# Distance matmuls cut from 97 rows by 512 columns to four of 25 rows by 256 columns, x and y on row tiles of their own

## The chip, the cores and the metric

The kernel runs on one core of a Trainium2 chip. A core has TensorE (PE, with its weight loads shown apart as PEld), VectorE (DVE), ScalarE (ACT), GpSimd (POOL) and SyncE (SP, which here only issues DMAs). The metric is the device time of one execution in microseconds (us), as the median of several runs. The profile is one execution of its own, with its own time.

## The reference

The input is x of 4 images, 32x32 pixels, 128 channels. Three stages follow one another for every image, each added onto x:

```
x = x + conv(_gn(x))          # deformable convolution, 8 groups, 9 points, 32 channels per group
t = t + attn(_ln_t(t))        # slice attention over the 1024 tokens, 8 heads
t = t + ffn(_ln_t(t))         # top-2 of 8 experts, 128 -> 512 -> 128, gelu

# in conv, for each pixel, group g and point k:
px, py = ww + deform[..., 0], hh + deform[..., 1]
samp = gather(y0, x0) * wy0 * wx0 + gather(y0, x0 + 1) * wy0 * wx1 + ...   # 4 corners
out  = einsum('bhwgkc,bhwgk->bhwgc', samp, weights) @ out_w + out_b
```

## The kernel before, in words

The gather is done without addresses. For one set (a position in the token order together with a group) and a sampled point, the weight of grid column q is relu(1 - |px - q|), and the same for rows with py. So the kernel needs for every point its distance to each of the 32 grid lines, in x and in y. The step `distances(k)` makes these distances on PE: the positions, split into three bf16 parts whose sum is the f32 value, are the stationary operand (`lp`, 97 rows: 3 parts times 32 sets, and a row of ones), and a constant 0/1 matrix (`spread_b`, with minus the grid number in its last row, as 1 - q) is the moving operand. One matmul gives 16 sets times 32 grid lines for 128 points: one bank of PSUM (512 f32 columns). There is one for x (bank 4) and one for y (bank 5).

The work is a loop over 4 images x 8 groups x 4 batches x 2 halves, so k runs from 0 to 255. For each k:

- PE: `distances(k + 3)` (line 731), then side work, then `products(n, pair)` of k (line 743, 32 f32 matmuls of 36 rows x 64 columns, which the profile counts as 64), and after every eighth k `contract` (line 758, 128 f32 matmuls on 32x32 tiles, counted as 256); one k later `project` (line 766) of the group before.
- ACT: `take_x` (line 1031, reads bank 4), side work, two `x_ramps` (line 1041), which `products` waits for.
- DVE: `take_y` (line 1331, reads bank 5), side work, `take` (line 1339, copies the products out).
- POOL: two `ysb` products (line 655) from what `take_y` wrote.
- SP: `load_group` brings the next group's positions (line 452), weights (459) and values (466) from DRAM, where `store_parts` (439) put the positions of a whole image.

The side work is written out by hand by slot numbers (`PREP_SLOTS`, `ATTENTION_SLOTS`, `TILE_SLOT` and so on): under image 0's groups runs the preparation of images 1 to 3, under those of image 1 to 3 the attention and the experts of the image before. On PE it stands between `distances(k + 3)` and `products` of k, and nearly all of it is matmuls with 128 rows and 128 columns of weights. The last image's attention and experts follow the loop. Every engine runs its queue in order; semaphores tie them. Ahead of the loop stands a prologue in which POOL makes the constants (line 593 is the 0/1 pattern of `spread_b`) and DVE finishes them (1186, 1190); ACT starts only after them.

A "height" below is the tile height with which a matmul sets up the 128x128 array: with up to 32 rows, up to 64, or all 128.

Of the kernel before, what the change touches and what calls it, by code (L numbers as in the profile page):

```python
# [30 lines left out]
ALU = mybir.AluOpType  # L31
# [18 lines left out]
LROWS = PARTS * SETS + 1  # L50
# [90 lines left out]
def conv_attn_moe(nc, t_in, out):  # L141
# [3 lines left out]
    with ExitStack() as ctx:  # L145
        def sb(name, shape, dt=F32):
            return ctx.enter_context(nc.sbuf_tensor(name, shape, dt))
# [9 lines left out]
        parts_dram = nc.dram_tensor("position_parts", [B, PARTS, P, G * 2 * P], BF16, kind="Internal").ap()  # L157
# [47 lines left out]
        spread_b = sb("spread_b", [P, SETS, GRID], BF16)  # L205
# [50 lines left out]
        spread_f = early[:, N:2 * N].rearrange("p (s q) -> p s q", s=SETS)  # L256
# [123 lines left out]
        def _(sp):  # L380
# [56 lines left out]
            def store_parts(b):  # L437
                sp.wait_ge(s.parts_ready, b + 1)
                sp.dma_start(parts_dram[b].rearrange("r p n -> p r n"), parts).then_inc(s.parts_stored, 16)
# [5 lines left out]
            def load_group(ig):  # L445
# [5 lines left out]
                for r in range(PARTS):  # L451
                    sp.dma_start(lp[r * SETS:(r + 1) * SETS, ig % 2, :, :, :].rearrange("p b d n -> p b (d n)"),
                                 parts_dram[b][r].rearrange("(b p) (g n) -> g p b n", b=BATCHES, g=G)[g])\
                      .then_inc(parts_loaded[ig % 2], 16)
# [105 lines left out]
        def _(pl):  # L560
# [29 lines left out]
            for r in range(PARTS):  # L590
                if r:
                    pl.wait_ge(s.constants_made, 15 + r)
                pl.affine_select(out=spread_f, in_=spread_f, compare_op=ALU.not_equal, fill=1.0, base=-SETS * r,
                                 pattern=[[-1, SETS], [0, GRID]], channel_multiplier=1).then_inc(s.constants_made, 1)
            block_diagonal(head_mask, DH, 18)
            for q in range(4):
                if q:
                    pl.wait_ge(s.constants_made, 20 + q)
                v = head_pick[:, :].rearrange("p (j g) -> p j g", g=S)
                pl.affine_select(out=v, in_=v, compare_op=ALU.not_equal, fill=1.0, base=-32 * q,  # L600
                                 pattern=[[-S // HG, HG], [0, S]], channel_multiplier=1).then_inc(s.constants_made, 1)
# [67 lines left out]
        def _(pe):  # L669
# [52 lines left out]
            def distances(k):  # L722

                n, half = k // 2, k % 2
                ig, beta = n // BATCHES, n % BATCHES
                if beta == 0 and half == 0:
                    pe.wait_ge(parts_loaded[ig % 2], 16 * PARTS * (ig // 2 + 1))
                for d, bank, taken, done in ((0, X_BANK, s.x_taken, s.dx_summed), (1, Y_BANK, s.y_taken, s.dy_summed)):
                    if k:
                        pe.wait_ge(taken, k)  # L730
                    pe.matmul(ps[:, bank, :], lp[0:LROWS, ig % 2, beta, d, :],  # L731
                              spread_b[0:LROWS, half * CHUNK:(half + 1) * CHUNK, :].rearrange("p s q -> p (s q)"),
                              start=True, stop=True).then_inc(done, 1)
# [224 lines left out]
            pe.wait_ge(s.constants_made, 24)  # L958
# [197 lines left out]
        def _(dve):  # L1156
# [10 lines left out]
            def small_constants():  # L1167
                dve.memset(eps_col[:, :], EPS).then_inc(s.small_constants, 1)
                dve.wait_ge(s.constants_made, 18)
# [15 lines left out]
                last = PARTS * SETS  # L1185
                chain(s.small_constants, dve.tensor_scalar(
                    spread_f[last:last + 1, :, :],
                    grid_i[last:last + 1, :].rearrange("p (o q) -> p o q", o=1).broadcast_to([1, SETS, GRID]),
                    -1.0, 1.0, ALU.mult, ALU.add), 9)
# [448 lines left out]
```

## Time and profile before

| | |
|---|---|
| median of 3 runs | 1552.92 us (1536.53 to 1554.06) |
| profiled execution: its time, its span | 1547.26 us, 1544.8 us |
| PE busy, and mean granted clock | 1215.9 us (79%), 0.796 of 2.4 GHz |
| DVE, ACT, POOL busy | 904.8, 733.5, 693.5 us |
| chain that ended last | PE 61%, DVE 21%, issue 8%, POOL 5% |

The chain is the one to read for what a change is worth: it leads back from the last instruction, at each step to what released it. A busy share is only how much an engine had to do. The granted clock is 1.2 or 2.4 GHz at any moment, so the same instructions stand in the trace with two lengths.

### The profile page before, as it was taken

How to read it: one execution, taken by the hardware profiler on the slowest of the kernel's cores; microseconds unless marked ns; L12 is line 12 of the kernel's file. 1: busy time of each engine (PE TensorE's matmuls, PEld its weight loads, DVE VectorE, ACT ScalarE, POOL GpSimd, SP SyncE). 2: the span in 40 equal slices, each digit the busy share in tenths (PEclk: the TensorE clock that was granted, in tenths of full speed). 3: DMA queues.
4: the chain of work that ended last, by engine and by line, in shares of the span. 5: the costliest groups of instructions: out<-in, count | busy, mean ns of one | idle time of the engine just before them, and what ended most of it. 6: DMA issues, size and time to landing. Idle time of an engine off the chain costs nothing.

```text
span 1544.8 us, 63235 instructions
## 1 busy us (share of the span) xinstructions
PE 1215.9 (79%) x28236; PEld 943.8 (61%) x28236; DVE 904.8 (59%) x1619; ACT 733.5 (47%) x1403; POOL 693.5 (45%) x674
## 2 busy tenths in 40 slices
PE   3297785987898789998977889998877899865391
PEld 2165564665556568886565668875565688735291
DVE  4468578686768556446767454457785644464311
ACT  1255363553565256665553347665543566422060
POOL 4155455454443564347533744466335644420303
PEclk9568695795897668997996569997977899986596
DMA  5502213122000321552111224621103235200761
GB/s 137 136 25 52 79 40 78 60 58 79 25 27 22 88 83 58 149 146 68 30 35 44 68 69 124 182 86 42 38 11 98 73 108 163 83 18 0 243 178 53
DMA packets 166288, 121.96 MB, mean 79 GB/s; under 512 B 45641, under 2 KB 146050, under 8 KB 165506
## 3 DMA queue, kind: packets, MB, share of 16 engines
q1 hardware_dynamic: 161922, 109.53, 25.3%
q0 software_dynamic: 4096, 8.40, 1.8%
q8 instruction: 222, 3.64, 1.0%
q14 instruction: 48, 0.39, 0.1%
HBM read 89.38 MB, written 28.51 MB: 76 GB/s over the span
## 4 chain that ended last, share of the span: by engine, by line
PE 61%; DVE 21%; issue 8%; POOL 5%; ACT 2%; DMA 1%; SPq 0%; DVEq 0%; POOLq 0%; ACTq 0%
PE ps L743 15%; PE ps L758 14%; PE ps L731 7%; PE ps L918 5%; PE ps L931 5%; DVE asb L1339 4%; PE ps L766 3%; DVE yr L1331 2%; POOL ysb L655 1%; DVE x_tok L1348 1%; POOL picked L633 1%; DVE region L1297 1%; PE ps L787 1%; PE ps L841 1%; PE ps L696 1%
## 5 line engine op out<-in xcount | busy, mean ns | idle before, releaser
L655 POOL TENSOR_TENSOR ysb<-yr,rw 128x512 f32<-128x512 f32 x512 | 552.5, 1102 | 629.7 <-DVE yr L1331 549.9
L743 PEld LDWEIGHTS ps<-xsb,ysb 36*64 36x64 f32 x16384 | 324.6, 160 | 148.0 <-issue 120.5
L743 PE MATMUL ps<-xsb,ysb 36*64 36x64 f32 x16384 | 363.7, 249 | 58.0 <-DVE x_tok L1348 34.2
L1339 DVE COPY asb<-ps 128x1024 f32<-128x1024 f32 x256 | 312.3, 1220 | 163.3 <-PE ps L743 161.6
L1041 ACT ACTIVATE xsb<-xr,pick 128x512 f32<-128x512 f32 x512 | 361.7, 764 | 4.4
L1331 DVE TENSOR_SCALAR yr<-ps 128x512 f32<-128x512 f32 x256 | 174.3, 681 | 223.0 <-PE ps L731 217.6
L758 PE MATMUL ps<-asb,vd 32*32 32x256 f32 x8192 | 212.2, 465 | 63.4 <-DVE asb L1339 50.7
L731 PE MATMUL ps<-spread_b,lp 97*128 97x512 bf16 x512 | 190.4, 452 | 57.4 <-DVE yr L1331 28.6
L1031 ACT ACTIVATE xr<-ps 128x512 f32<-128x512 f32 x256 | 152.0, 594 | 172.5 <-PE ps L731 172.0
L758 PEld LDWEIGHTS ps<-asb,vd 32*32 32x32 f32 x8192 | 153.5, 114 | 116.1 <-issue 88.0
L1048 ACT ACTIVATE osp<-ps 128x256 f32<-128x256 f32 x128 | 39.6, 402 | 274.8 <-PE ps L758 274.8
L1116 ACT ACTIVATE region<-ps,b_col 128x128 f32<-128x128 f32 x368 | 105.4, 370 | 89.2 <-PE ps L918 89.2
L623 POOL DMA_INDIRECT sorted_rows<-region,row_no x64 | 62.9, 983 | 119.1 <-DVE row_no L1519 103.4
L633 POOL DMA_INDIRECT picked<-expert_rows,row_no x64 | 61.5, 960 | 91.3 <-DMA expert_rows<-region 74.5
L731 PEld LDWEIGHTS ps<-spread_b,lp 97*128 97x128 bf16 x512 | 32.7, 100 | 102.0 <-DVE yr L1331 38.2
L918 PEld LDWEIGHTS ps<-region,ring 128*128 128x128 f32 x616 | 81.3, 196 | 9.8 <-issue 1.6
L918 PE MATMUL ps<-region,ring 128*128 128x128 f32 x616 | 84.4, 281 | 1.5 <-issue 1.5
L931 PE MATMUL ps<-ring,region 128*128 128x128 f32 x616 | 82.5, 277 | 0.0
L931 PEld LDWEIGHTS ps<-ring,region 128*128 128x128 f32 x616 | 76.2, 194 | 0.4
L1557 DVE COPY region<-ps 128x128 f32<-128x128 f32 x92 | 26.8, 291 | 76.3 <-PE ps L931 76.3
L766 PEld LDWEIGHTS ps<-outw,osp 128*128 128x128 f32 x512 | 65.1, 200 | 6.5 <-ACT osp L1048 1.8
L766 PE MATMUL ps<-outw,osp 128*128 128x128 f32 x512 | 65.3, 283 | 1.3 <-ACT osp L1048 1.3
(232 smaller groups left out, 1097.4 us busy)
## 6 DMA issues: line engine op xcount, KB each, us to landing
ring<-in_L_ffn_W SPq DMA_DIRECT2D x154, 256.0 KB, 3.3
vd<-group_values SPq DMA_DIRECT2D x128, 128.0 KB, 2.7
asb<-in_L_ffn_W SPq DMA_DIRECT2D x30, 256.0 KB, 4.5
position_parts<-region SPq DMA_DIRECT2D x4, 1536.0 KB, 5.8
lp<-position_parts SPq DMA_DIRECT2D x96, 64.0 KB, 2.6
group_values<-region SPq DMA_DIRECT2D x32, 128.0 KB, 3.4
weight_rows<-region SPq DMA_DIRECT2D x4, 1024.0 KB, 4.3
rw<-weight_rows SPq DMA_DIRECT2D x32, 128.0 KB
```

What stands on the lines that cost most here:

```text
L655: pl.tensor_tensor(ysb[:, n % 2, pair * CHUNK:(pair + 1) * CHUNK, u, :], yr[:, k % 3, :, :], rw[:, ig % 2, u, first:first + CHUNK].rearran ...
L731: pe.matmul(ps[:, bank, :], lp[0:LROWS, ig % 2, beta, d, :], spread_b[0:LROWS, half * CHUNK:(half + 1) * CHUNK, :].rearrange("p s q -> p ( ...
L743: last = pe.matmul(o[:, :, NV * q:NV * q + NV], ysb[rows, n % 2, col, :, :].rearrange("p u y -> p (u y)"), xsb[rows, n % 2, col, :, :], st ...
L758: last = pe.matmul(ps[32 * jc:32 * jc + 32, j, 0:256], vd[rows, ig % 2, x, :], asb[rows, x, :, :, :].rearrange("p i n m -> p (i n m)"), st ...
L766: last = pe.matmul(pcol(2, t), osp[:, t, :], outw[:, ig % G, :], start=True, stop=True)
L918: last = pe.matmul(ps[:, hidden_bank(b, i), j * P:(j + 1) * P], ring_part(r, 0)[:, j * P:(j + 1) * P], xsT[:, i, :], start=True, stop=True)
L931: last = pe.matmul(ps[:, expert_bank(b, i), 0:C], hT[:, i % 2, j, :], ring_part(r, 1)[:, j * P:(j + 1) * P], start=(j == 0), stop=(j == HJ ...
L1031: act.activation(xr[:, half * CHUNK:(half + 1) * CHUNK, :].rearrange("p s q -> p (s q)"), ps[:, X_BANK, :], ACT.Relu, bias=1.0, scale=-1.0 ...
L1041: act.activation(xsb[:, n % 2, sets, :, v], xr[:, sets, :], ACT.Relu, bias=pick[:, v:v + 1], scale=-1.0).then_inc(s.x_ready, 1)
L1116: last = act.activation(hT[:, i % 2, j, :], ps[:, hidden_bank(b, i), j * P:(j + 1) * P], ACT.Gelu, bias=b1_col[:, i, j:j + 1])
L1331: dve.tensor_scalar(yr[:, k % 3, :, :].rearrange("p s q -> p (s q)"), ps[:, Y_BANK, :], 0.0, 1.0, ALU.max, ALU.min).then_inc(s.y_taken, 1)
L1339: dve.tensor_copy(asb[:, :, :, 2 * beta + pair, :].rearrange("p x i m -> p i x m"), ps[:, 2 * pair:2 * pair + 2, :].rearrange("p i (x m) - ...
```

## The change

Each pair of distance matmuls becomes four. x and y of a half of 16 sets no longer hold all 97 rows; each has a strip of 25 rows (8 sets x 3 parts and the row of ones) which starts at partition 0, 32, 64 or 96, and is multiplied by a 25-row constant into 256 columns. x and y of the same 8 sets stand in neighbouring strips, one behind the other in the queue, and write different banks. The positions lie in DRAM so that the three parts of a set are neighbours, and a group is loaded with eight DMAs of 24 partitions in place of three of 32. The constant is made for four strips (twelve selects of 256 columns in place of three of 1024).

```diff
-LROWS = PARTS * SETS + 1
+OCT = 8
+LROWS = 1 + PARTS * OCT
-        parts_dram = nc.dram_tensor("position_parts", [B, PARTS, P, G * 2 * P], BF16, kind="Internal").ap()
+        parts_dram = nc.dram_tensor("position_parts", [B, P, PARTS, G * 2 * P], BF16, kind="Internal").ap()
-        spread_b = sb("spread_b", [P, SETS, GRID], BF16)
+        spread_b = sb("spread_b", [P, OCT, GRID], BF16)
-                sp.dma_start(parts_dram[b].rearrange("r p n -> p r n"), parts).then_inc(s.parts_stored, 16)
+                sp.dma_start(parts_dram[b], parts).then_inc(s.parts_stored, 16)
-                for r in range(PARTS):
-                    sp.dma_start(lp[r * SETS:(r + 1) * SETS, ig % 2, :, :, :].rearrange("p b d n -> p b (d n)"),
-                                 parts_dram[b][r].rearrange("(b p) (g n) -> g p b n", b=BATCHES, g=G)[g])\
-                      .then_inc(parts_loaded[ig % 2], 16)
+                for half in range(2):
+                    for d in range(2):
+                        first = 32 * (2 * half + d) + 1
+                        for o in range(2):
+                            sp.dma_start(lp[first:first + PARTS * OCT, ig % 2, :, o, :],
+                                         parts_dram[b].rearrange("(b h o m) r x -> (b h o m r) x", h=2, o=2, m=OCT)
+                                         .rearrange("(b h o z) (g d n) -> h g d o z b n", h=2, o=2, z=PARTS * OCT, g=G,
+                                                    d=2)[half, g, d, o]).then_inc(parts_loaded[ig % 2], 16)
...
-            for r in range(PARTS):
-                if r:
-                    pl.wait_ge(s.constants_made, 15 + r)
-                pl.affine_select(out=spread_f, in_=spread_f, compare_op=ALU.not_equal, fill=1.0, base=-SETS * r,
-                                 pattern=[[-1, SETS], [0, GRID]], channel_multiplier=1).then_inc(s.constants_made, 1)
+            for i in range(4 * PARTS):
+                pl.wait_ge(s.constants_made, 15 + i)
+                pl.affine_select(out=spread_f, in_=spread_f, compare_op=ALU.not_equal, fill=1.0,
+                                 base=-(32 * (i // PARTS) + 1 + i % PARTS), pattern=[[-PARTS, OCT], [0, GRID]],
+                                 channel_multiplier=1).then_inc(s.constants_made, 1)
...
-                    pe.wait_ge(parts_loaded[ig % 2], 16 * PARTS * (ig // 2 + 1))
-                for d, bank, taken, done in ((0, X_BANK, s.x_taken, s.dx_summed), (1, Y_BANK, s.y_taken, s.dy_summed)):
-                    if k:
-                        pe.wait_ge(taken, k)
-                    pe.matmul(ps[:, bank, :], lp[0:LROWS, ig % 2, beta, d, :],
-                              spread_b[0:LROWS, half * CHUNK:(half + 1) * CHUNK, :].rearrange("p s q -> p (s q)"),
-                              start=True, stop=True).then_inc(done, 1)
+                    pe.wait_ge(parts_loaded[ig % 2], 16 * 8 * (ig // 2 + 1))
+                if k:
+                    pe.wait_ge(s.x_taken, k)
+                    pe.wait_ge(s.y_taken, k)
+                for o in range(2):
+                    for d, bank, done in ((0, X_BANK, s.dx_summed), (1, Y_BANK, s.dy_summed)):
+                        rows = slice(32 * (2 * half + d), 32 * (2 * half + d) + LROWS)
+                        last = pe.matmul(ps[:, bank, o * OCT * GRID:(o + 1) * OCT * GRID], lp[rows, ig % 2, beta, o, :],
+                                         spread_b[rows, :, :].rearrange("p s q -> p (s q)"), start=True, stop=True)
+                        if o:
+                            last.then_inc(done, 1)
...
-                last = PARTS * SETS
-                chain(s.small_constants, dve.tensor_scalar(
-                    spread_f[last:last + 1, :, :],
-                    grid_i[last:last + 1, :].rearrange("p (o q) -> p o q", o=1).broadcast_to([1, SETS, GRID]),
-                    -1.0, 1.0, ALU.mult, ALU.add), 9)
+                for row in range(0, P, 32):
+                    last = dve.tensor_scalar(spread_f[row:row + 1, :, :], across(grid_i, OCT)[row:row + 1, :, :],
+                                             -1.0, 1.0, ALU.mult, ALU.add)
+                chain(s.small_constants, last, 9)
```

The order of PE's queue where attention stands under image 1's groups. Before (L731 distances, L743 products, L766 the projection, L806 attention's projection, L823 and L824 its logits):

```order
L731 MATMUL ps<-spread_b,lp 128x512 [waits x_taken]
L731 MATMUL ps<-spread_b,lp 128x512 [waits y_taken]
L766 MATMUL ps<-outw,osp 128x128 [waits out_copied]
L766 MATMUL ps<-outw,osp 128x128 x7
L806 MATMUL ps<-wxT,region 128x256 [waits rtemp_ready]
L806 MATMUL ps<-wxT,region 128x256 x3
L743 MATMUL ps<-xsb,ysb 64x32x2 [waits conv_added,y_ready,x_ready]
L743 MATMUL ps<-xsb,ysb 64x32x2 x31
```

The same place now (L739 distances, L752 products, L775 projection, L815 attention's):

```order
L739 MATMUL ps<-spread_b,lp 128x256 [waits y_taken,x_taken]
L739 MATMUL ps<-spread_b,lp 128x256 x3
L775 MATMUL ps<-outw,osp 128x128 [waits out_copied]
L775 MATMUL ps<-outw,osp 128x128 x7
L815 MATMUL ps<-wxT,region 128x256 [waits rtemp_ready]
L815 MATMUL ps<-wxT,region 128x256 x3
L752 MATMUL ps<-xsb,ysb 64x32x2 [waits conv_added,y_ready,x_ready]
L752 MATMUL ps<-xsb,ysb 64x32x2 x31
```

Nothing has changed its place; two distance matmuls are four of half the columns, and the first of them carries both waits.

SP's queue at the first group, before:

```order
L439 DMA position_parts<-region 128x3x2048 [waits parts_ready]
L443 DMA weight_rows<-region 128x2048 [waits rows_copied]
L452 DMA lp<-position_parts 32x4x256 [waits parts_stored]
L452 DMA lp<-position_parts 32x4x256 x2
L459 DMA rw<-weight_rows 128x256 [waits rows_stored]
```

and now:

```order
L440 DMA position_parts<-region 128x6144 [waits parts_ready]
L444 DMA weight_rows<-region 128x2048 [waits rows_copied]
L456 DMA lp<-position_parts 24x4x128 [waits parts_stored]
L456 DMA lp<-position_parts 24x4x128 x7
L464 DMA rw<-weight_rows 128x256 [waits rows_stored]
```

Eight loads of positions stand ahead of the load of the weights, with 256 bytes in a row in place of 512.

## Rows read from the trace of the kernel before

**Rows 1.** The page: span, and busy time of each engine (share, instructions)

```profile
span 1544.8 us, 63235 instructions
PE 1215.9 (79%) x28236; PEld 943.8 (61%) x28236; DVE 904.8 (59%) x1619; ACT 733.5 (47%) x1403; POOL 693.5 (45%) x674
```

**Rows 2.** The page: the chain that ended last, by engine and line

```profile
PE 61%; DVE 21%; issue 8%; POOL 5%; ACT 2%; DMA 1%; SPq 0%; DVEq 0%; POOLq 0%; ACTq 0%
PE ps L743 15%; PE ps L758 14%; PE ps L731 7%; PE ps L918 5%; PE ps L931 5%; DVE asb L1339 4%; PE ps L766 3%; DVE yr L1331 2%; POOL ysb L655 1%; DVE x_tok L1348 1%; POOL picked L633 1%; DVE region L1297 1%; PE ps L787 1%; PE ps L841 1%; PE ps L696 1%
```

**Rows 3.** Chain in order of time (start us, us, what), 539 to 543 us

```profile
539.59 0.97 PE ps L731 x2
540.55 1.92 PE ps L743 x64
```

**Rows 4.** The same, 644 to 650 us

```profile
645.10 0.54 PE ps L731 x2
645.64 0.89 PE ps L918 x8
646.53 0.89 PE ps L931 x8
647.43 1.09 PE ps L743 x64
```

**Rows 5.** Chain, first and last pairs of the three commonest kinds, with what follows

```profile
112.15 0.54 PE ps L731 x2
112.69 0.49 PE ps L696 x2
...
1331.84 0.54 PE ps L731 x2
1332.38 0.89 PE ps L918 x8
...
1181.29 0.97 PE ps L731 x2
1182.25 0.85 PE ps L886 x4
...
79.07 0.97 PE ps L731 x2
80.04 1.92 PE ps L743 x64
...
1198.30 0.97 PE ps L731 x2
1199.27 0.74 PE ps L743 x19
```

**Rows 6.** Chain, one contraction

```profile
552.57 7.21 PE ps L758 x236
```

**Rows 7.** PE, 763 to 767 us (start, us, engine, line, operation, out<-in, shape, count)

```profile
763.91 1.13 PE L823 MATMUL ps<-region,ws_bd 128*128 128x512 f32 x2
764.96 1.12 PE L824 MATMUL ps<-region,head_pick 32*128 32x512 f32 x2
766.01 1.16 PE L743 MATMUL ps<-xsb,ysb 36*64 36x64 f32 x64
```

**Rows 8.** Chain, 411 us: four f32 matmuls of 512 columns at one height

```profile
411.08 1.72 PE ps L787 x4
```

**Rows 9.** PE, 860 to 862 us: a matmul of 8 rows behind the distances

```profile
860.09 1.04 PE L731 MATMUL ps<-spread_b,lp 97*128 97x512 bf16 x2
861.05 0.79 PE L892 MATMUL ps<-b,region 8*128 8x128 f32 x2
```

**Rows 10.** PE, 805 to 807 us: products behind the distances

```profile
805.90 0.60 PE L731 MATMUL ps<-spread_b,lp 97*128 97x512 bf16 x2
806.43 0.75 PE L743 MATMUL ps<-xsb,ysb 36*64 36x64 f32 x36
```

**Rows 11.** Line 731: idle time of PE and PEld ahead of it (us, times)

```profile
  DVE yr L1331: 66.8, 38
  ACT xr L1031: 35.4, 25
```

**Rows 12.** Who waited for whom (us, times, longest): products on ACT

```profile
PEld ps L743 <- ACT xsb L1041: 18.3, 20, 1.6
```

**Rows 13.** Timeline of the prologue, POOL and DVE, then ACT

```profile
1.39 0.30 POOL L565 MEMSET vbias<- 128x256 f32 x1
1.64 0.94 POOL L566 MEMSET asb<- 128x1024 f32 x1
9.92 4.09 POOL L593 TENSOR_SCALAR_AFFINE_SELECT asb<-asb 128x1024 f32<-128x1024 f32 x3
14.04 0.28 DVE L1170 CAST count<-asb 128x32 f32<-128x32 int32 x1 [13.09 <-POOL asb L593]
14.70 1.98 POOL L600 TENSOR_SCALAR_AFFINE_SELECT head_pick<-head_pick 128x128 f32<-128x128 f32 x4
15.75 0.77 DVE L1186 TENSOR_SCALAR asb<-asb 1x1024 f32<-1x1024 int32 x1
16.55 1.02 ACT L1000 ACTIVATE region<-ps 128x1024 f32<-128x1024 f32 x1 [6.69 <-DVE asb L1186]
```

**Rows 14.** Timeline, first two loads of positions and the first distances

```profile
64.45 2.48 SPq L452 DMA_DIRECT2D lp<-position_parts  x3
69.36 1.01 PE L731 MATMUL ps<-spread_b,lp 97*128 97x512 bf16 x2 [6.38 <-DMA lp<-position_parts]
70.65 1.37 SPq L452 DMA_DIRECT2D lp<-position_parts  x3
```

**Rows 15.** Line 452: who waited for it, and time to landing

```profile
  PE ps L731: 6.4, 1
DMA to landing us min/median/max: 1.9/2.6/5.8
```

**Rows 16.** Windows: length, busy us of PE, PEld, DVE, ACT, POOL, then PEclk, DMA share, GB/s

```profile
76.00:92.00 16.00, 16.00 (x344) 11.81 (x343) 10.75 (x16) 12.05 (x19) 11.88 (x12) 0.50 0.06 15
196.00:216.00 20.00, 17.23 (x489) 12.33 (x488) 19.35 (x30) 15.19 (x23) 13.88 (x14) 1.00 0.07 21
644.60:651.40 6.80, 6.80 (x176) 6.13 (x170) 4.22 (x6) 5.79 (x15) 2.97 (x3) 1.00 0.54 158
```

More of the change, by code:

```diff
@@ L255, in conv_attn_moe @@
         grid_i = early[:, 6 * G * K:6 * G * K + GRID].bitcast(I32)
-        spread_f = early[:, N:2 * N].rearrange("p (s q) -> p s q", s=SETS)
+        spread_f = early[:, N:N + OCT * GRID].rearrange("p (s q) -> p s q", s=OCT)
         at[0] = 0
@@ L588, in _ @@
             pl.memset(turn_flat, 0.0).then_inc(s.constants_made, 1)
-            for r in range(PARTS):
-                if r:
-                    pl.wait_ge(s.constants_made, 15 + r)
-                pl.affine_select(out=spread_f, in_=spread_f, compare_op=ALU.not_equal, fill=1.0, base=-SETS * r,
-                                 pattern=[[-1, SETS], [0, GRID]], channel_multiplier=1).then_inc(s.constants_made, 1)
-            block_diagonal(head_mask, DH, 18)
+            for i in range(4 * PARTS):
[3 more added lines that the diff above has]
+                                 channel_multiplier=1).then_inc(s.constants_made, 1)
+            block_diagonal(head_mask, DH, 27)
             for q in range(4):
                 if q:
-                    pl.wait_ge(s.constants_made, 20 + q)
+                    pl.wait_ge(s.constants_made, 29 + q)
                 v = head_pick[:, :].rearrange("p (j g) -> p j g", g=S)
@@ L957, in _ @@
                 prepare(0, step)
-            pe.wait_ge(s.constants_made, 24)
+            pe.wait_ge(s.constants_made, 33)
             pe.wait_ge(s.grid_chain, 2)
@@ L1168, in small_constants @@
                 dve.memset(eps_col[:, :], EPS).then_inc(s.small_constants, 1)
-                dve.wait_ge(s.constants_made, 18)
+                dve.wait_ge(s.constants_made, 27)
                 dve.tensor_copy(count[:, :], grid_i).then_inc(s.small_constants, 1)
```

## The prediction

> **What bounds the kernel now.** The busy shares come first [rows 1]: PE is busy 79% of the span and no other engine over 59%, so nothing but PE can be near its limit, yet a share says nothing of order. The chain of waits does [rows 2]: 61% of it is work of PE and 21% of DVE; the distance matmuls (L731) hold 7%, about 110 us. Read in order of time, the chain shows two speeds of the same step. At 538 us, where PE does only distances and products, a pair of distances takes 0.97 us and the products 1.92 [rows 3]; at 645 us, with the experts between, the pair takes 0.54 and the products 1.09 [rows 4]. The windows say why: the granted clock is 0.50 of full speed in the one kind of stretch and 1.00 in the other [rows 16].
>
> Followed piece by piece, the chain goes through 173 of the 256 pairs, and they differ by speed and by what stands behind them (the first and the last of each kind stand in [rows 5]): 120 pairs of 0.54 us ahead of a 128-row matmul, 26 of 0.97 ahead of such a one, 17 of 0.97 ahead of products. The other ten are 3 of 0.54 ahead of products, 1 of 0.54 and 2 of 0.97 ahead of the 8-row matmul L892, and 3 and 1 (by speed) where the chain leaves PE. What the change is worth depends on this list.
>
> **The columns.** A pair streams 1024 columns. At half the clock they take twice as long, so 0.97 - 0.54 = 0.43 us is their time at 2.4 GHz, and 0.11 is left, which the clock hardly moves [rows 3, 4]. The change streams as many columns, but x and y may run side by side: 512 column steps, if they do. That they do is likely. The 64 products, with halves of rows and of columns as tiles, take 1.09 us; eight 128-column f32 matmuls take 0.89, so 64 of 64 columns would take 3.6 one by one [rows 4]: more than three run at once. In a contraction 256 matmuls of 256 columns take some 7.3 us (236 recorded in 7.21), where one by one they would need 256 x 0.22 = 56 [rows 6]: over seven at once, and one strip of 32 rows has only four tiles of 32 columns, so strips overlap too. So a pair gets shorter by 0.21 us at 2.4 GHz and 0.43 at 1.2; its ends are 0 (one after the other) and these.
>
> **The change of height.** Against this stands something that the diff does not show. Before, the distances have 97 rows and the array is set up for 128, as for nearly all the side work behind them; the side work's first weights are loaded under the distances. Now the distances are set up for 32 rows, and the array is set up anew before the side work. The trace has this step in attention: L824 has 32 rows and stands behind L823 with 128. From L823 to L824 it is 1.05 us, from L824 to the products again 1.05 [rows 7]. Each is two passes of 512 columns, and four such passes at one height take 1.72 [rows 8], two 0.86: each of the two changes of height costs 0.19 us, weights not loaded ahead among it. At 1.2 GHz I take 0.30, between 0.19 and twice that; the 8-row matmul there starts 0.96 us after the distances, 0.10 over the two passes' 0.86, and its own weights then take time too [rows 9]. Ahead of products nothing is added: from distances to products the height changes today as well (0.53 us at 2.4 GHz, 0.10 over the columns) [rows 10]. Nor from products to distances.
>
> Sum over the chain: 120 x (0.21 - 0.19) = 2.4; 26 x (0.43 - 0.30) = 3.4; 20 slow pairs without a new change (17, 2, 1) x 0.43 = 8.6; 7 fast ones x 0.21 = 1.5. Together **16 us gained**. The ends: with no charge for the height 127 x 0.21 + 46 x 0.43 = 46 gained; without overlap 120 x 0.19 + 26 x 0.30 = 31 lost. Off the chain the shorter pairs are worth nothing.
>
> **The waits.** The x matmul now waits for `take_y` as well. y held up the queue before, so PE stands as long as ever (66.8 us for DVE ahead of line 731) [rows 11]; but ACT gets x later in these cases, and with it `take_x`, its side work and the ramps, which are needed three steps on. Products waited 18.3 us for ACT in all [rows 12]. I take 2 us lost, ends 0 and 10. y is there 0.2 us sooner after the pair starts, which helps DVE where it waits; that is in the shortened pairs already.
>
> **Prologue.** POOL made three selects of 1024 columns in 4.09 us (1.36 each) and four of 128 in 1.98 (0.50 each) [rows 13]: 0.97 ns per column and 0.37 fixed, so twelve of 256 take 12 x 0.62 = 7.4, 3.3 more. The memset of the same tile falls from 0.94 to about 0.30, as for another tile of 256 columns. DVE's row of ones becomes four short instructions (0.77 us together, perhaps 1.0). ACT's first copy waits for all this, and the preparation for ACT: **2.8 us later** (0 to 4). Then the first distances wait for the positions. Five more issues at 1.37 / 3 = 0.46 us [rows 14] are 2.3 us; the first three took 0.83 each, which is the upper end, 4.1; if the last lands no sooner, all of it counts. I take **2.3**. Later groups load about a group ahead, and PE waited for this load once only, at the start [rows 15], so SP's five further issues in each of 31 groups are hidden by it; if a load were late, each group would pay some 2 us.
>
> The positions now move in rows of 256 bytes in place of 512. The Trainium skill ("DMA: Bandwidth & Descriptors", Specifications) states that below 512 bytes a DMA engine reads, modifies and writes. By that the first landing of 2.6 us would be longer, perhaps doubled by an estimate from the row, and the sum 2.6 us more; no row here shows such a load of positions, and I leave it out.
>
> **The clock.** From 76 to 92 us PE never pauses, with products, distances and little else, and is granted 0.50; from 644 to 651 it never pauses either, with the experts' 128-row matmuls in it, and is granted 1.00; from 196 to 216, with the preparation woven in, it is granted 1.00 at 17.2 busy of 20 [rows 16]. So the low clock goes with narrow work, not with pauses alone, and the change makes the distances narrow: 25 rows in place of 97. Stretches that hold 2.4 GHz today with preparation or attention may lose it. If the one from 196 to 216 did, its 17.2 busy us would be 34.4 in place of 20: 14 us. I take one such, **14 us lost**, with 0 and three (43) as ends.
>
> **The sum.** 1547.3 (the profiled execution's own time, span 1544.8) - 16 + 2 + 5 + 14 = 1552.3. That execution lies 5.7 below the median of the three runs; their spread of 17.5 us is wider than this, and I make no correction. **Forecast 1552 us: no change.** A change of 2% (31 us) is about what a measurement of this kernel can tell.
>
> **Rivals.**
>
> 1. The change of height costs nothing here, and the clock holds. For it: between distances and products a change of height costs only 0.10 us [rows 10], so side work might pay as little or less. Against it: L824 pays it twice in [rows 7]. Then 1547 - 46 + 2 + 5 = 1508, faster by 2.6 to 2.9%. Chance 0.13. The Trainium skill ("TensorE: Matmul & The Clock Gate", Measured speedup vs the span model) gives 3.07 times for four 32-row tiles side by side and no charge for what stands between; by it alone this rival would be the forecast. The rows on overlap agree with it, rows 7 do not agree that it is the whole price.
>
> 2. The clock falls in several stretches, not one. Place: image 0's groups with preparation, and attention's under images 1 to 3. Price: 43 us or more. 1547 - 16 + 7 + 45 = 1583, slower. It decides from about three stretches of 20 us on. For it: narrow work at 0.50 without a pause [rows 16]. Against: contractions and 128-row side work stand in every group and are as they were. Chance 0.15.
>
> 3. x and y run one after the other. Then the pair keeps its length and the height is paid: 1547 + 31 + 7 = 1585 with no change of clock. Against it: the overlap in [rows 4, 6]. Chance 0.06.
>
> 4. The pairs leave the chain and DVE or the later waits take what is gained, with nothing lost at the clock: 1547 to 1555, the same verdict as the forecast. Chance 0.12, and 0.54 for the forecast itself.
>
> **Numbers.** Forecast and rival 4 are within 2%: 0.66, and a part of rivals 2 and 3 ends there as well (0.03), as does a part of 1 (0.01). Faster 0.12, same 0.70, slower 0.18. The range leaves out rival 1 and the far part of 2 and 3: 1528 (forecast's terms at their good ends, 1547 - 16 + 2, and a run as low as the lowest) to 1583.
>
> **What would show it.** Four distance matmuls, the first two starting within some hundredths of a us, a pair on the chain of about 0.33 us at 2.4 GHz and 0.54 at 1.2: overlap is right. Two of them 0.11 or 0.21 apart: rival 3. The first side matmul behind the distances standing about 0.2 us longer than now: the change of height. ACT's first copy near 19.3 us and the first distances near 74.5: the prologue. The granted clock of 196 to 216 and its kind, and the mean against 0.796: the clock term; a mean under 0.75 is rival 2. What would make the forecast wrong first is the clock, whose term is the least sure and the largest range.

## The result: 1.0% slower

The changed kernel takes 1557.78 us (median of 20 runs, 1544.95 to 1567.24), the kernel before 1540.63 beside it (20 runs, 1529.65 to 1554.06): ratio **1.0104, 95% interval 1.0084 to 1.0124**. The forecast was no change, with a sum of +5 us; measured is a loss of 17 us, small and clear of the noise. That 1552 and 1558 us lie so near each other is partly luck: the sum started from an execution of 1547.3, which was 7 us above the median that the kernel before has here. An execution can fall into a slower state of the chip; the three that did in the runs below are left out of every ratio and every clock.

First the page of the changed kernel, in the order of [rows 1] and [rows 2]: span, busy time of each engine, chain by engine and line, then the distances' own row (out<-in, shapes, count | busy us, mean ns | idle before).

```profile
span 1553.4 us, 64664 instructions
PE 1209.7 (78%) x28748; PEld 952.0 (61%) x28748; DVE 904.1 (58%) x1622; ACT 733.8 (47%) x1403; POOL 692.5 (45%) x683
...
PE 60%; DVE 22%; issue 9%; POOL 5%; ACT 2%; DMA 1%; SPq 1%; POOLq 0%; DVEq 0%; ACTq 0%
...
L739 PE MATMUL ps<-spread_b,lp 25*128 25x256 bf16 x1024 | 119.0, 317 | 72.8 <-DVE yr L1339 44.4
```

The distances hold 4% of the chain in place of 7%: about 44 us have gone from there (110 us before, 67 now), and the span is 8.6 longer. So a gain was had and lost elsewhere. The chain of the changed kernel at the place of [rows 4] shows the gain and the first thing that takes it (start us, us, what; L927 and L940 are the experts' matmuls that were L918 and L931, L752 the products):

```profile
644.60 1.09 PE ps L752 x64
645.69 0.32 PE ps L739 x4
646.02 1.09 PE ps L927 x8
647.10 0.89 PE ps L940 x8
```

The pair is down from 0.54 to 0.32, and the eight matmuls behind it are up from 0.89 to 1.09. In each profile some 43 cycles of the chain have just this form (distances, eight, eight, 64 products, distances); from start to start they take 3.416 us before and 3.397 now (medians), 0.019 less. At 1.2 GHz the pair fell from 0.97 [rows 3] to 0.54, and what stands behind it grew too. First before, then now, the same four matmuls (L903, now L912):

```profile
573.46 0.97 PE ps L731 x2
574.43 0.85 PE ps L903 x4
```

```profile
578.29 0.54 PE ps L739 x4
578.83 1.04 PE ps L912 x4
```

The prologue, as in [rows 13, 14]: twelve selects, four rows of ones, the first loads, the first distances.

```profile
9.46 6.91 POOL L597 TENSOR_SCALAR_AFFINE_SELECT asb<-asb 128x256 f32<-128x256 f32 x12
16.40 0.28 DVE L1179 CAST count<-asb 128x32 f32<-128x32 int32 x1 [15.46 <-POOL asb L597]
18.15 1.40 DVE L1195 TENSOR_SCALAR asb<-asb 1x256 f32<-1x256 int32 x4
66.75 4.58 SPq L456 DMA_DIRECT2D lp<-position_parts  x8
72.88 0.61 PE L739 MATMUL ps<-spread_b,lp 25*128 25x256 bf16 x4 [7.59 <-DMA lp<-position_parts]
```

The first distances start at 72.88 in place of 69.36, 3.5 us later. And the granted clock, in windows as in [rows 16]; the last two windows are long ones, the same of the changed kernel and, in the second fence, of the kernel before (the column behind POOL is PEclk):

```profile
79.00:95.00 16.00, 15.61 (x383) 12.57 (x385) 10.45 (x17) 12.79 (x20) 12.02 (x12) 0.50 0.17 48
196.00:216.00 20.00, 17.74 (x440) 13.27 (x440) 18.37 (x28) 14.21 (x23) 12.97 (x13) 0.83 0.09 21
644.60:651.40 6.80, 6.80 (x169) 6.01 (x168) 4.22 (x6) 5.81 (x15) 2.29 (x3) 1.00 0.77 222
...
85.00:350.00 265.00, 209.42 (x5804) 159.78 (x5800) 194.84 (x245) 133.74 (x214) 136.24 (x112) 0.74 0.23 57
1050.00:1350.00 300.00, 263.86 (x6433) 207.10 (x6432) 181.15 (x319) 159.62 (x317) 142.41 (x139) 0.79 0.27 76
```

```profile
85.00:350.00 265.00, 211.80 (x5667) 156.95 (x5669) 195.31 (x244) 131.55 (x211) 136.59 (x112) 0.78 0.22 57
1050.00:1350.00 300.00, 259.43 (x6671) 203.69 (x6663) 183.05 (x321) 157.79 (x314) 146.49 (x144) 0.87 0.27 78
```

The two extremes of [rows 16] are where they were; the stretch from 196 to 216 lost a part of its 2.4 GHz (1.00 to 0.83), and the long stretches lost a little each: 0.78 to 0.74, and 0.87 to 0.79 in the last third. The mean went from 0.796 to 0.771. A single stretch of 20 us says little by itself: in a second execution of each kernel (section F) the same 20 us have 0.80 before and 0.67 now.

### The profile page after: what moved, and what is told of

The parts are those of the page before. It is cut to its first block, busy times and chain, and to the rows that moved or that the text cites. A ratio compares the mean times of both kernels' runs of the same rounds, so it can differ in the third digit from the quotient of the medians.

```text
span 1553.4 us, 64664 instructions
## 1 busy us (share of the span) xinstructions
PE 1209.7 (78%) x28748; PEld 952.0 (61%) x28748; DVE 904.1 (58%) x1622; ACT 733.8 (47%) x1403; POOL 692.5 (45%) x683
## 4 chain that ended last, share of the span: by engine, by line
PE 60%; DVE 22%; issue 9%; POOL 5%; ACT 2%; DMA 1%; SPq 1%; POOLq 0%; DVEq 0%; ACTq 0%
PE ps L752 15%; PE ps L767 14%; PE ps L927 6%; PE ps L940 5%; PE ps L739 4%; DVE asb L1347 4%; PE ps L775 4%; DVE yr L1339 3%; POOL ysb L660 1%; PE ps L796 1%; POOL picked L638 1%; DVE x_tok L1356 1%; DVE region L1305 1%; PE ps L850 1%; PE ps L912 1%
## 5 line engine op out<-in xcount | busy, mean ns | idle before, releaser
L752 PE MATMUL ps<-xsb,ysb 36*64 36x64 f32 x16384 | 376.9, 255 | 63.4 <-DVE x_tok L1356 29.9
L752 PEld LDWEIGHTS ps<-xsb,ysb 36*64 36x64 f32 x16384 | 337.1, 166 | 139.4 <-issue 111.5
L1040 ACT ACTIVATE xr<-ps 128x512 f32<-128x512 f32 x256 | 152.6, 596 | 201.3 <-PE ps L739 200.2
L767 PEld LDWEIGHTS ps<-asb,vd 32*32 32x32 f32 x8192 | 157.2, 115 | 104.9 <-issue 76.5
L739 PE MATMUL ps<-spread_b,lp 25*128 25x256 bf16 x1024 | 119.0, 317 | 72.8 <-DVE yr L1339 44.4
L739 PEld LDWEIGHTS ps<-spread_b,lp 25*128 25x128 bf16 x1024 | 31.0, 96 | 108.4 <-issue 78.9
L927 PE MATMUL ps<-region,ring 128*128 128x128 f32 x616 | 89.0, 289 | 0.0
L927 PEld LDWEIGHTS ps<-region,ring 128*128 128x128 f32 x616 | 76.2, 195 | 11.7 <-issue 11.2
L940 PE MATMUL ps<-ring,region 128*128 128x128 f32 x616 | 82.3, 276 | 0.8 <-issue 0.8
L940 PEld LDWEIGHTS ps<-ring,region 128*128 128x128 f32 x616 | 75.5, 193 | 1.5 <-issue 1.4
L775 PE MATMUL ps<-outw,osp 128*128 128x128 f32 x512 | 70.6, 295 | 1.3 <-ACT osp L1057 1.3
L775 PEld LDWEIGHTS ps<-outw,osp 128*128 128x128 f32 x512 | 64.2, 204 | 8.7 <-issue 6.9
```

The lines of the kernel that those rows point to most:

```text
L739: last = pe.matmul(ps[:, bank, o * OCT * GRID:(o + 1) * OCT * GRID], lp[rows, ig % 2, beta, o, :], spread_b[rows, :, :].rearrange("p s q - ...
L752: last = pe.matmul(o[:, :, NV * q:NV * q + NV], ysb[rows, n % 2, col, :, :].rearrange("p u y -> p (u y)"), xsb[rows, n % 2, col, :, :], st ...
L767: last = pe.matmul(ps[32 * jc:32 * jc + 32, j, 0:256], vd[rows, ig % 2, x, :], asb[rows, x, :, :, :].rearrange("p i n m -> p (i n m)"), st ...
L775: last = pe.matmul(pcol(2, t), osp[:, t, :], outw[:, ig % G, :], start=True, stop=True)
L927: last = pe.matmul(ps[:, hidden_bank(b, i), j * P:(j + 1) * P], ring_part(r, 0)[:, j * P:(j + 1) * P], xsT[:, i, :], start=True, stop=True)
L940: last = pe.matmul(ps[:, expert_bank(b, i), 0:C], hT[:, i % 2, j, :], ring_part(r, 1)[:, j * P:(j + 1) * P], start=(j == 0), stop=(j == HJ ...
```

## The experiments

Each kernel is compared by its ratio to the kernel before, run beside it on the same chip. That kernel took about 1594 us on some of the chips used and 1540 on others, so microseconds of different chips are not compared. "Clock" is the mean granted clock over a kernel's timed runs.

### A. The rows of the distances alone, both ways

```diff
-pe.matmul(ps[:, bank, :], lp[0:LROWS, ig % 2, beta, d, :], spread_b[0:LROWS, ...
+pe.matmul(ps[:, bank, :], lp[0:P, ig % 2, beta, d, :], spread_b[0:P, ...
```

On the kernel before; rows 97 to 127 meet zeros in spread_b. 

> The kernel before, with the distance matmuls over all 128 rows in place of 97; rows 97 to 127 of the constant are zero, so the result is the same, and so are the columns, the height, the order and the waits. Theory clock (the change loses its time because the narrower distances bring a lower granted clock): wider distances bring a higher one, mean granted clock 0.81 to 0.83 in place of 0.796, time 8 to 20 us below the kernel before. Rival waits and heights (the lost time is the change of height, the joint wait and the prologue; the clock only follows from the pauses): nothing here is different, within 3 us of the kernel before.

The counterpart: 65 rows (the ones in row 64), which leaves the third part of each position out of the sum. 

> The kernel before, with the row of ones moved to row 64 and the distance matmuls over rows 0 to 64 in place of 97 rows; left out of the positions is their third bf16 part. Same columns, height, order, waits and loads. Theory clock: mean granted clock 0.78 or below, time 5 to 15 us above the kernel before, with pairs of the same length at the same clock. Rival waits and heights: within 3 us of the kernel before.

Measured: 128 rows **0.9947** (0.9923 to 0.9971), clock 0.801; 65 rows **1.0129** (1.0085 to 1.0174), clock 0.770; before 0.788 beside them. Columns, array setup and waits are the same in all three, and the duration of one matmul is too (first 97 rows, before; then 65):

```profile
L731 PE MATMUL ps<-spread_b,lp x512: 376/390/634, 69.4 to 1332.0; 97*128 97x512 bf16 x171
```

```profile
L731 PE MATMUL ps<-spread_b,lp x512: 376/389/634, 68.3 to 1362.4; 65*128 65x512 bf16 x171
```

Minimum, median and maximum do not move, so a matmul costs no more for its rows; what moves is the granted clock, and with it the time of the whole program. Fewer rows alone, 65 in place of 97, cost 1.3%, 21 us. Both moved the way that the reading by the clock had them, and by more than the 3 us of its rival: 8 us less (8 to 20 expected) and 21 more (5 to 15 expected).

### B. Wider products, on both kernels

```diff
-rows = slice(64 * i, 64 * i + AK)
+rows = slice(64 * i, 64 * i + 64)
```

AK is 36; the further rows hold zeros on one side of each product. 

> The kernel before, with the products over 64 rows in place of 36 (rows 36 to 63 of their operand are zero, so the result is the same; tile, columns and count are the same). Theory clock: the narrowest of PE's work becomes wider and the stretches at 1.2 GHz with distances and products get 2.4; mean clock 0.88 or more, 40 to 100 us faster. Rival waits and heights: within 5 us of the kernel before.

> The changed kernel with the same edit to the products. Theory clock: with the clock held up in both, what is left between this and the kernel before with that edit is the prologue (3.5 us in the traces), the joint wait (0 to 2) and the pairs (some 5 us gained at 2.4 GHz): -3 to +5 us, in place of the 17 measured without it. Rival waits and heights: the gap stays at 15 to 20 us.

Measured: before with it **0.9791** (0.9749 to 0.9834), clock 0.846; changed with it **0.9911** (0.9876 to 0.9946), clock 0.820. Both gain from rows that add nothing. The first gains less than expected (33 us at 0.846, for 40 to 100 us at 0.88 or more). The distance between the two did not shrink, as the second expectation wanted: 19 us. What it is made of was open until F.

### C. Full height in the changed kernel

Four constants, spread_b[P, 4, OCT, GRID], each with its own strip of 32 rows and zeros elsewhere, and matmuls over 128 rows; loads, joint wait and selects as in the change. x and y no longer overlap. 

> The changed kernel with its layout, its eight loads, its twelve selects and its joint wait, but each distance matmul over all 128 rows: the constant stands four times, zero outside one strip, so the result is the same. Gone are the change of height, the overlap of x and y and the narrow rows; what stays of the change is prologue, loads and wait. Its fair partner is the kernel before over 128 rows (ratio 0.995 to the kernel before). Theory clock plus heights: ratio to the kernel before 0.997 to 1.001, 3 to 8 us above that partner. Rival loads and wait (eight small loads or the joint wait cost in the loop): 1.005 or more, as much as the change itself.

Measured: **1.0038** (1.0011 to 1.0066), clock 0.799, against 0.9947 and 0.801 of the 128 rows in A, which has the same height and nearly the same clock. So the joint wait, loads, prologue and split matmuls together cost 0.9% (give or take 0.4), 14 us, where my terms had 7. Of these, 6.6 stood already at the first copy to asb (85.4 us against 78.8), more than the change's own 3.3, since this kernel's constants are larger.

This run also tests the change of height. With full height the pair is back at 0.54 us, and the eight matmuls behind it are back at 0.89 from the 1.09 of the changed kernel:

```profile
641.34 0.54 PE ps L738 x4
641.88 0.89 PE ps L926 x8
```

### D. Tiles of 64 rows

x on rows 0 to 48, y on 64 to 112, four matmuls of 64 columns of sets by 512, four loads and six selects. 

> The distances on 64x64 tiles: x in rows 0 to 48, y in rows 64 to 112, each for 16 sets and 512 columns, each in two halves of 64 weight columns, all four side by side; four loads of 48 partitions. The column time is that of the change (512 steps), but the tile is that of the products, so no change of height comes in. Theory clock plus heights: the pairs gain some 45 us on the chain (0.21 and 0.43 us each), narrow rows lose about two thirds of what the change loses by the clock (17 us): 20 to 35 us faster than before, ratio 0.98 to 0.987, mean clock near 0.78. Rival (only the clock counts, lengths of pairs do not reach the end): slower than before, 1.003 to 1.008.

The same with 64 rows in distances and products. 

> The same with distances and products over 64 rows in place of 49 and 36 (the rest zero, same result). Theory clock plus heights: both gains add, ratio 0.94 to 0.965, mean clock 0.83 or more. Rival (only the clock counts): as the kernel before with wide products, 0.975 to 0.985.

And the kernel before with 128 rows in the distances and 64 in the products. 

> The kernel before with distances over 128 rows and products over 64, nothing else. Theory clock: the two gains (0.995 and 0.979) add, 0.970 to 0.977, mean clock 0.85. If the clock is already as high as the pauses allow, no more than the wide products alone, 0.979.

Measured: **1.0008** (0.9977 to 1.0040), clock 0.766; **0.982** (0.9768 to 0.9873), clock 0.829; **0.979** (0.9742 to 0.9838), clock 0.851. The first two missed their expectations. The pairs got even shorter than forecast, but a tile of 64 rows does not spare the change of height, as the expectation had it: the side work still has 128 rows, and it pays the same 0.20 us. In the first:

```profile
648.82 0.22 PE ps L738 x4
649.04 1.09 PE ps L927 x8
```

Its clock is 0.024 below that of the kernel before, which by the relation at the end of F goes with 17 us. As an estimate: the distances' part of the chain is 54 us shorter (56 in place of 110), the height takes 29 (0.20 at the 146 pairs with side work behind them), the clock 17, and the joint wait, which this kernel has too, up to 7. Together that is about nothing, as measured. The third kernel has hardly more than the 64-row products of B, in time (0.979 and 0.9791, each give or take 0.5%) and in clock (0.851 and 0.846). Where the products have 64 rows, 31 more rows in the distances no longer bring the 0.013 of clock that they brought in A.

### E. The joint wait, the order, the loads and the selects, one by one

On the kernel before, both waits ahead of the x matmul:

```diff
-for d, bank, taken, done in (...):
-    if k:
-        pe.wait_ge(taken, k)
+if k:
+    pe.wait_ge(s.x_taken, k)
+    pe.wait_ge(s.y_taken, k)
+for d, bank, done in (...):
```

> The kernel before with one edit: both waits (x taken, y taken) stand ahead of the x matmul of each distances step, as the change has them; tiles, heights, loads and prologue are as before. Theory A (the middle of the span is longer by the clock alone): the joint wait costs 0 to 3 us, ratio 1.000 to 1.002, and ACT's idle time on the distances stays near 172 us. Theory B (the joint wait holds x back behind DVE's reading of y, and this is the 8 to 11 us that the change loses between the first and the last asb copy): ratio 1.005 to 1.008, and ACT's idle time on the distances rises towards the 200 us that the changed kernel has.

On the changed kernel, `for o in range(2)` moved inside the loop over x and y, each with its own wait: 

> The changed kernel with the order x, x, y, y in place of x, y, x, y, each pair behind its own wait: the joint wait is gone, and with it the overlap of x and y. Theory B: what the joint wait costs comes back and more than pays for the overlap, ratio to before 1.003 to 1.008 (the changed kernel has 1.010). Theory A: the overlap is lost (0.1 to 0.2 us for up to 256 steps, those of them on the chain), the clock stays as low as in the changed kernel, ratio 1.010 to 1.020.

On the kernel before, each load cut by x or y and by half of the batches: 

> The kernel before with its 3 loads of position parts for each image group cut into 12, each with x or y alone (runs of 256 bytes as in the change, which has 8 loads for a group). Theory C (small loads, their issue on SP and the queue behind them cost the time): the first distances start 1 to 3 us later and the ring and value loads behind them come later too, ratio 1.004 to 1.010. Theories A and B: the first group's loads cost 1 to 3 us once, everything else lies ahead of its use, ratio 1.000 to 1.002.

On the changed kernel, 12 selects with base=-1000 behind its own: 

> The changed kernel with 12 further selects on POOL behind its own 12, which fill nothing: 12 x 0.59 us = 7.1 us more ahead of the constants that DVE waits for. Theory D (the prologue's selects are on the path and come back in full at the end of the span): 7 us over the changed kernel, ratio to before 1.014 to 1.016. If the prologue has slack, or later stages take the delay up: ratio as the changed kernel, 1.008 to 1.012.

Measured: joint wait **1.0048** (1.0015 to 1.0081); own waits **1.0170** (1.0126 to 1.0213); 12 loads **1.0046** (1.0014 to 1.0079); 24 selects **1.0156** (1.0104 to 1.0207). The joint wait shows where it was looked for, in who waited for the distances: ACT stands at 215.9 us with it, and at 195.5 in the kernel with 12 loads, on the same chip and with the old waits (the last two columns: us, times). PE itself stands no longer ahead of the distances: 145.5 us with it, 142.9 with 12 loads (sums over all that it waited for).

```profile
  DVE yr L1332: 224.3, 34
  ACT xr L1032: 215.9, 87
```

```profile
  DVE yr L1333: 227.3, 34
  ACT xr L1033: 195.5, 83
```

The 12 loads show in the chain twice, at 670 and at 1011 us, where the experts' ring weights stand behind them on SP; at the first place:

```profile
670.33 1.39 SPq L454
674.12 1.47 SPq L454
679.63 4.36 DMA ring<-in_L_ffn_W
```

No row of SP or of a DMA stands in the changed kernel's chain from 73 to 1360 us: nine further loads reach the path, its five did not visibly. And 3.8 us of the 7 that 12 loads cost arise before the loop is in step: its first distances start at 72.1 us, those of the joint-wait kernel on the same chip at 68.3.

Own waits were expected to lose the overlap of x and y. They did not. Where x and y are both taken in time, the pair has the length of the changed kernel's, and the trace shows x and y starting within 10 ns of each other, as there:

```profile
645.02 0.33 PE ps L738 x4
645.35 1.09 PE ps L926 x8
```

So this run sheds the joint wait alone. It is not faster than the change (1.0104, and 1.0159 in F), at a clock of 0.754, the lowest of all kernels here: what the joint wait costs on the kernel before is not seen to come back when it is taken out of the changed one. Why is not known. The 24 selects put the first copy to asb at 90.3 us in place of 83.6, 6.7 of the 7.1 us added; since the changed kernel itself has 1.0104 or 1.0159, the ratio alone tells nothing.

### F. The clock given back to the changed kernel

The products' slice of B with 54 in place of 64. The changed kernel itself and the kernel before ran with it, for their profiles on this chip. 

> The changed kernel as it is, on the chip of the other experiments of this call, as their yardstick: 1.010 as in its first comparison (1.008 to 1.013). The parts measured one by one on the kernel before are 0.5% for the joint wait, 0.5% for twelve loads in place of three, and 1.3% for lower distances; the changed kernel gets the overlap back.

> The changed kernel with products over 54 rows in place of 36 (rows 36 to 53 hold zeros on one side of each product), and nothing else: distances, waits, loads and prologue stay as in the change. 18 rows more in 64 products a step make up in rows x columns for what the distances lost. Theory A (clock): the granted clock comes back from 0.77 to near the 0.80 of before, and the ratio to before falls by about 1.3 points, from 1.010 to 0.995 to 1.001. Theory E (the clock is a bystander; waits, loads and prologue make up the whole of the change's cost): ratio stays at 1.007 to 1.012 whatever the clock shows.

> The kernel before as it is, for its profile on this chip: ratio 1.00 within what one round tells, clock 0.79 to 0.80; the tail behind the last asb copy some 20 us longer than in the first profile, as in the profiles of all kernels of these runs.

Measured: changed **1.0159** (1.0118 to 1.0200), clock 0.763; with 54 rows **0.9931** (0.9908 to 0.9955), clock 0.812; before 1.0002 (0.9965 to 1.0040), clock 0.805. The change itself is slower here than in its first comparison, above the 1.008 to 1.013 expected. Nothing but rows of zeros turned 1.6% slower into 0.7% faster, 2.3 points where 1.3 were expected; the products' matmuls keep their length (212/219/367 ns with 54 rows, 212/219/368 with 36: minimum, median, maximum). PEclk in 40 slices, changed, changed with 54 rows, and before:

```profile
PEclk9558566685689566998787669996876699986596
```

```profile
PEclk9558696696798668998997699988977699986595
```

```profile
PEclk9578786785797667998996669997977899986596
```

The changed kernel is lower in most slices of the first third and of the last. The first copy to asb comes at 79.3 us before, 82.8 changed and 83.0 with 54 rows, the last at 1336.3, 1362.2 and 1328.9. So the prologue costs 3.5 in both, and the rest of the 26 us arose between and is gone with 54 rows.

Then the same edit on the kernel before, and 64 rows on both once more. 

> The kernel before with products over 54 rows in place of 36, as e14 did with the changed kernel. Theory A (clock): the kernel before gains less by it than the changed kernel did (2.3 points), since its clock is higher to begin with; ratio 0.982 to 0.990, clock 0.82 to 0.83. If it gains as much (ratio 0.977 to 0.980), the change costs the same 1 to 1.5% at any clock and theory A is wrong in its size.

> The changed kernel with products over 64 rows, once more, on the chip where 54 rows gave 0.9931. Theory A: the clock rises a little over that run's 0.81, ratio 0.983 to 0.992. The first run had 0.9911.

> The kernel before with products over 64 rows, once more, beside e18. The first run had 0.9791. Theory A: ratio 0.976 to 0.982, and the distance to e18 is what the change costs where the clock is high in both: between 0 and 0.5% by the sum of the prologue, the joint wait, the loads and the overlap. If it is 1.2% again, waits and loads cost more at a high clock than the sum has them.

Measured: before with 54 rows **0.9858** (0.9831 to 0.9886), clock 0.827; changed with 64 **0.9896** (0.9857 to 0.9936), clock 0.821; before with 64 **0.9813** (0.9782 to 0.9845), clock 0.842. The kernel before gains 1.4 points from 54 rows, the changed one 2.3 (on another chip, of the faster kind). The gap at 64 rows is 0.8 points (1.2 in B), above the 0 to 0.5 expected, at clocks that are still 0.02 apart.

**What a hundredth of the clock goes with.** The runs of one kernel differ in clock too. Over 103 runs of the kernel before on five chips, each taken against its chip's mean, the time falls by **7.0 us per 0.01 of clock** (correlation -0.70). By this, in B 0.026 go with 18 us of the 19 between the kernels, in F 0.022 with 15 of 13, and at 36 rows 0.042 with 30 of 25; with 54 rows, where the changed kernel has 0.007 more than before, 5 of the 11 us it is faster. So the gap at 64 rows is, as far as this relation carries, the clock again. It is a relation, not an experiment: a run with more pauses may be granted less, and then part of the slope runs that way.

## Why the prediction was wrong

**Pairs: right.** The change does what it says. A pair takes 0.32 and 0.54 us (0.33 and 0.54 forecast), and the change of height puts 0.20 on the side work behind it (0.19 forecast), so rivals 1 and 3 are out. At 2.4 GHz with the experts the two cancel to 0.019 us, as the sum's 0.21 - 0.19 had it. At 1.2 GHz the height costs 0.19 too (0.85 to 1.04), where 0.30 was taken; by the sum's 26 pairs that is 3 us in favour. (The contraction of [rows 6] is 7.8 us when scaled to 256 matmuls, not 7.3; over seven at once still holds.) The 16 us as a whole were not measured alone. An estimate: the full-height kernel of C stands 6 us above the kernel before at a clock 0.009 higher, so some 13 at the same clock; the changed kernel in F stands 25 above at a clock 0.042 lower, with which 30 go, so some 5 below. The difference of 18 us, less 2 for C's larger constants, is what the pairs are worth: about 16, uncertain by 8.

The Trainium skill ("TensorE: Matmul & The Clock Gate", Measured speedup vs the span model) has a speedup for tiles side by side and no charge for what stands between. The first part fits here (1024 columns in the time of 512). By the second alone rival 1 would have been right, and that is not borne out: 0.20 us of each pair's 0.21 go to the work behind it at the full clock.

**Prologue: right in kind, 3.5 us in place of 5.1.** ACT's first copy came 3.0 us later (19.58 against 16.55; 2.8 forecast), the selects taking 0.58 each (6.91 / 12; 0.62 forecast). The loads then added only 0.5, where 2.3 was taken: eight issues took 2.1 us more than three (4.58 and 2.48), but the distances started 1.55 us after the last issue in place of 2.43. So rows of 256 bytes did not make the landing longer, which was the open point of the prediction.

**Loads of later groups: taken at nothing.** Cutting three loads into twelve costs 0.46% (0.14 to 0.79), 7 us. Of these 3.8 belong to the first group, which is the prologue's matter; the rest, some 3, fits the ring loads that stand behind them on SP, a queue the prediction looked at for lp alone. For the change's eight this is an upper bound; its chain shows none of it.

**The joint wait: 2 us forecast, 7 measured on the kernel before** (0.48%; 2 to 13), within the ends of 0 and 10 and above the value taken. The argument was that PE stands as long as ever. It does, on that kernel (145.5 and 142.9 us in E): but ACT gets x later. In the changed kernel the price is not shown: own waits brought nothing back. Who waited for the distances, before and changed:

```profile
  DVE yr L1331: 217.6, 34
  ACT xr L1031: 172.0, 91
```

```profile
  DVE yr L1339: 213.5, 34
  ACT xr L1040: 200.2, 95
```

DVE waits 4 us less, ACT 28 more. Not all of the 28 can be the joint wait's: with own waits ACT still waits 200.2 us (on a slower chip), and with the joint wait and 54-row products 179.8, where the changed kernel beside it has 206.3. So this wait is longer at a lower clock as well (0.812 and 0.763).

**The clock: this is the step that failed.** The idea was right, that narrower distances are granted less; the term's place and size were not. It took one stretch, 196 to 216, lost whole, and 14 us. That stretch lost a third of what was forecast (0.83, not 0.50), and in its place many stretches lost a little. Rival 2 had the right place and the wrong price: it asked for whole stretches at 0.50 and a mean under 0.75; the mean fell to 0.771. What a hundredth of clock costs has three readings: 65 rows in place of 97 on the kernel before, 1.3% (0.9 to 1.7), 21 us for 0.019, so 11 us (7 to 15); 54-row products in the changed kernel, 35 us for 0.049, so 7.1; and the relation's 7.0. No run takes the 97 rows down to the change's 25 with all else equal. With 7.0, from 0.796 (the profile before) or 0.805 (the same kernel in F) to the first comparison's 0.769, the term is 19 to 25 us; in F, from 0.805 to 0.763, it is 30.

Put together: -16 for the pairs, 0 to 7 for the joint wait, 3.5 for the prologue, 0 to 3 for the loads. That is -12.5 to -2.5, and with the clock 6.5 to 22.5 us in the first comparison, where 17 were measured, and 17.5 to 27.5 in the second, where 25 were. The forecast had +5. Of the 12 us missing in the first comparison, 5 to 11 are the clock's and at most 5 the joint wait's; of the 20 in the second, 16 are the clock's. How the clock's part and the waits' part overlap is not settled: the joint wait alone ran at 0.788 against 0.790, so a part of its price may be the clock's as well.

Both kernels are beaten: by the kernel before with 64-row products (0.9791 and 0.9813), and, keeping the change, by wider products (0.9931 with 54 rows, 0.9911 and 0.9896 with 64).

## What to carry to other kernels

Rows of a matmul that cost no time of their own may still hold the clock up; before you save rows on TensorE, compare the mean granted clock of a version with the rows alone taken away, and of one with rows of zeros added, since the second is an edit of one line, and the first of a few. Packing small matmuls side by side is worth less where what follows has another height: look at the first instruction behind them, which took all but a tenth of the gain here at 2.4 GHz and somewhat under half at 1.2. And a wait that is joined for two consumers is to be priced also at the one that used to go first, not only at the engine that waits.

## What was not expected of the hardware

The time of one matmul does not depend on its rows (376/390/634 ns at 97 rows and 376/389/634 at 65), but 32 rows fewer in 512 such matmuls cost 1.3% of a 1594 us program, at a mean granted clock of 0.770 in place of 0.788, and 18 or 28 rows of zeros in each of the products (16384 in the profile's count) gained 1.4 and 2.1%, at 0.827 and 0.846. With 64-row products already there, 128-row distances brought no more that can be seen (0.9791 and 0.979, clock 0.846 and 0.851).

Going from tiles of 32 rows to matmuls of 128 cost 0.20 us at the first of these (eight f32 ones, 0.89 to 1.09) at 2.4 GHz, and as much from tiles of 64 rows; it was gone at full height, with all else as in the change. At 1.2 GHz it was 0.19 us (0.85 to 1.04), so this price hardly depends on the clock, while the columns' time doubles.
